# Keys and values spread to the score and value matmuls three phases ahead, keys by way of DRAM, values from SBUF to SBUF, and a one-instruction normalisation on GpSimd

## The reference

```python
# L0: pre-norm, causal self attention, cross attention, MLP
x = x + sdpa(split(ln(x, g1, b1) @ w_qkv.T), causal) @ w_prj1.T + b_prj1
x = x + sdpa(ln(x, g2, b2) @ w_q.T, ctx @ w_kv.T) @ w_prj2.T + b_prj2
x = x + gelu(ln(x, g3, b3) @ w_fc1.T + b_fc1) @ w_fc2.T + b_fc2
# L1: rms norm, rotary q and k, cross attention
x = x + sdpa(rope(rms(x) @ Wq.T), rope(ctx @ Wk.T), ctx @ Wv.T) @ Wo.T
# L2: post-norm, masked scores
x = ln(x + mha(x, x, causal) @ Wo1 + bo1, g1, b1)
x = ln(x + mha(x, ctx, mask) @ Wo2 + bo2, g2, b2)
x = ln(x + gelu(x @ W1 + bf1) @ W2 + bf2, g3, b3)
# L3: as L0 without a causal mask, norms without gain and bias
```

## Time and profile before

| | |
|---|---|
| runs (median) | 2578.21 us (2570.23 to 2578.39) |
| profiled execution, its own time | 2566.47 us |
| its span, first to last instruction | 2564.4 us |
| mean granted TensorE clock | 0.967 of 2.4 GHz |
| PE / PEld / DVE / ACT / POOL busy | 89 / 75 / 72 / 65 / 54 % |
| DMA | 231.55 MB, 90 GB/s, q1 30.4% of 16 engines |

### The profile page before, as it was taken

One profiled execution on the slowest core, in us unless ns is written; L12 is line 12 of the kernel. 1 busy time (PEld: TensorE's weight loads), 2 busy tenths in 40 slices (PEclk: granted clock), 3 DMA queues, 4 the chain that ended last, 5 costly groups with the idle time before them and its releaser, 6 DMA issues.

```text
span 2564.4 us, 98727 instructions
## 1 busy us (share of the span) xinstructions
PE 2276.3 (89%) x37613; PEld 1919.4 (75%) x37613; DVE 1852.0 (72%) x4653; ACT 1657.8 (65%) x2884; POOL 1390.3 (54%) x3557
## 2 busy tenths in 40 slices
PE   2689888999998897999999988899999989799987
PEld 2478776788887776778887777778888877678875
DVE  3368776777777777778776777677777777677863
ACT  0256654778776664677776765477777766467775
POOL 3244334877554433688654443487755543377843
PEclk6799999999999999999999999999999999999999
DMA  6133333333333333333333333333333322333321
GB/s 153 44 91 97 89 89 93 86 94 94 99 98 89 90 88 89 91 91 92 99 98 83 101 90 90 93 86 94 91 100 97 90 79 83 87 90 89 93 76 44
DMA packets 354629, 231.55 MB, mean 90 GB/s; under 512 B 151456, under 2 KB 295584, under 8 KB 354144
## 3 DMA queue, kind: packets, MB, share of 16 engines
q1 hardware_dynamic: 349152, 222.07, 30.4%
q10 hardware_dynamic: 4128, 1.65, 0.3%
q0 software_dynamic: 864, 1.28, 0.3%
HBM read 159.87 MB, written 65.01 MB: 88 GB/s over the span
## 4 chain that ended last, share of the span: by engine, by line
PE 34%; POOL 25%; issue 21%; DMA 13%; DVE 3%; SPq 2%; POOLq 1%; ACT 1%; DVEq 0%; ACTq 0%
DMA kv_dram<-qkv_rows 6%; PE ps_scores_t L825 6%; DMA k_slots<-kv_dram 6%; PE ps_out L813 5%; PE ps_scores L788 5%; PE ps_turn L873 3%; POOL x_bias L660 3%; PE ps_wide L895 3%; POOL pre_rstd L604 2%; POOL post_rstd L604 2%; PE ps_turn L878 2%; POOL post_normed L641 2%; POOL x L644 2%; PE ps_wide L853 2%; PE ps_wide L854 2%
## 5 line engine op out<-in xcount | busy, mean ns | idle before, releaser
L1118 DVE TENSOR_REDUCE row_max<-ps_scores 128x16 f32<-128x1024 f32 x448 | 548.6, 1224 | 444.1 <-PE ps_scores L788 259.4
L727 ACT ACTIVATE probs<-ps_scores_t 128x512 f32<-128x512 f32 x896 | 535.4, 598 | 168.0 <-PE ps_scores_t L825 165.8
L1124 DVE TENSOR_TENSOR shifted<-ps_scores,row_max 128x512 f32<-128x512 f32 x896 | 611.8, 683 | 16.0 <-issue 0.6
L825 PE MATMUL ps_scores_t<-ident,shifted 128*128 128x128 f32 x3584 | 572.9, 283 | 15.9 <-ACT probs L727 15.1
L788 PE MATMUL ps_scores<-k_slots,qkv_rows 32*64 32x256 f32 x7168 | 317.4, 409 | 200.4 <-DMA k_slots<-kv_dram 150.5
L717 ACT COPY pv_sb<-ps_out 128x256 f32<-128x256 f32 x448 | 167.1, 373 | 461.0 <-PE ps_out L813 458.0
L825 PEld LDWEIGHTS ps_scores_t<-ident,shifted 128*128 128x128 f32 x3584 | 398.5, 143 | 55.4 <-issue 21.6
L813 PEld LDWEIGHTS ps_out<-probs,v_ones 128*32 128x32 f32 x14336 | 278.6, 151 | 146.9 <-issue 146.9
L813 PE MATMUL ps_out<-probs,v_ones 128*32 128x64 f32 x14336 | 343.1, 237 | 4.8 <-issue 3.7
L788 PEld LDWEIGHTS ps_scores<-k_slots,qkv_rows 32*64 32x64 f32 x7168 | 108.9, 132 | 291.7 <-issue 195.6
L707 ACT COPY qkv_rows<-ps_wide 128x384 f32<-128x384 f32 x384 | 184.3, 480 | 132.8 <-PE ps_wide L863 129.2
(11 more groups left out here) (170 smaller groups left out, 4530.9 us busy)
## 6 DMA issues: line engine op xcount, KB each, us to landing
k_slots<-kv_dram SPq DMA_DIRECT2D x448, 256.0 KB, 3.0
kv_dram<-qkv_rows SPq DMA_DIRECT2D x384, 128.0 KB, 2.2
v_ones<-kv_dram SPq DMA_DIRECT2D x896, 32.0 KB, 2.6
kv_dram<-qkv_rows SPq DMA_DIRECT2D x128, 64.0 KB, 1.7
x_in<-in_x SPq DMA_DIRECT2D x64, 64.0 KB, 1.9
ctx_in<-in_ctx SPq DMA_DIRECT2D x64, 64.0 KB, 1.9
out<-x SPq DMA_DIRECT2D x64, 64.0 KB, 1.7
kv_dram<-zeros SPq DMA_DIRECT2D x4, 512.0 KB, 7.1
```

The costliest lines, as they stand in the source:

```text
L727: nc.scalar.activation(probs[:, u, :, :], ps_scores_t[:, :] .rearrange("p (h t) -> p h t", h=4), ACT.Exp, scale=SCALE).then_inc(probs_read ...
L825: ins = nc.tensor.transpose(ps_scores_t[:, h * P:(h + 1) * P], shifted[:, j % 2, u, h * P:(h + 1) * P], ident[:, :])
L1118: v.tensor_reduce(row_max[:, :].rearrange("p (g n) -> p g n", n=SLOTS), ps_scores[:, :, 0:256].rearrange("p g (n k) -> p g n k", k=LEN), A ...
L1124: v.tensor_tensor(shifted[:, j % 2, u, :].rearrange("p (g n k) -> p g n k", n=SLOTS, k=LEN), ps_scores[:, 2 * u:2 * u + 2, 0:256].rearrang ...
```

## The change

The phase constants: q, k and v are computed three phases ahead of the scores (QKV 2 to 3), turns four (TURN_IN 3 to 4), statistics six (STATS 4 to 6).

On SP, `spread` is split. `rows_out(j+QKV)` sends k's rows to DRAM (64 KB, now without v) and v by four DMAs from SBUF to SBUF (64 partitions by 1 KB each); `spread(j+QKV-1)`, ahead of it in the phase, waits for the k write of the phase before and reads the slots. v's rows are written by ACT into `v_rows`, which already holds the zeros and ones around them, in a ring of eight (FAR), and `v_ones` has the same layout, so that the 32 weight columns of a value matmul are adjacent. ACT's one copy becomes two. On DVE, half 1 of `shift` comes right after half 0. On POOL, `normalised` is a drain and one tensor_scalar with mean and inverse root as its two scalars. Two waits are added for the program's ends (POOL on turns_ready, PE on attn_ready).

```diff
-QKV, TURN_IN, STATS = 2, 3, 4
+QKV, TURN_IN, STATS = 3, 4, 6
...
-        qkv_rows = sb("qkv_rows", [P, RING, 3, P])
+        qk_rows = sb("qk_rows", [P, RING, 2, P])
+        v_rows = sb("v_rows", [P, FAR, 2, HEADS // 2, V_COLUMNS])
-        v_ones = sb("v_ones", [P, RING, 2, 32, HEADS // 2])
+        v_ones = sb("v_ones", [P, FAR, 2, HEADS // 2, V_COLUMNS])
...
+                def rows_out(r, j):
+                    c, f = j % RING, j % FAR
+                    rope = layer_of(j) == L1_CROSS
+                    if rope:
                         sp.wait_ge(rope_ready.sem, rope_ready.at(r, j))
+                    else:
+                        sp.wait_ge(rows_ready.sem, rows_ready.at(r, j, 1))
+                    sp.dma_start(k_rows(c)[:, K_HOME:], qk_rows[:, c, 1, :]).then_inc(k_written[c].sem, 16)
+                    if rope:
                         sp.wait_ge(rope_v_ready.sem, rope_v_ready.at(r, j))
                     else:
                         sp.wait_ge(rows_ready.sem, rows_ready.at(r, j))
+                    for e in range(2):
+                        for b in range(2):
+                            sp.dma_start(v_ones[64 * e:64 * e + 64, f, b, :, :], v_rows[64 * b:64 * b + 64, f, e, :, :]) \
+                                .then_inc(v_landed[f].sem, 16)
+
+                def spread(r, j):
+                    c = j % RING
+                    sp.wait_ge(k_written[c].sem, k_written[c].at(r, j))
                     sp.dma_start(k_slots[:, c, :, :], k_windows(c)).then_inc(k_landed[c].sem, 16)
...
                 def phase(r, j, this, following):
+                    if exists(r, j + QKV - 1):
+                        spread(r, j + QKV - 1)
                     if exists(r, j + QKV):
-                        spread(r, j + QKV)
+                        rows_out(r, j + QKV)
...
                 def normalised(r, j, norm, src, rms=False):
+                    pool.drain()
+                    if rms:
+                        return pool.tensor_scalar(norm.normed[:, b, :], src, norm.rstd[:, b:b + 1], None, ALU.mult)
+                    return pool.tensor_scalar(norm.normed[:, b, :], src, norm.mean_var[:, b, 0:1],
+                                              norm.rstd[:, b:b + 1], ALU.subtract, ALU.mult)
...
                 def copy_rows(r, j):
-                    nc.scalar.copy(qkv_rows[:, j % RING, :, :], ps_wide[:, 0:3 * P]
-                                   .rearrange("p (n t) -> p n t", t=P)).then_inc(rows_ready.sem, 1)
+                    nc.scalar.copy(qk_rows[:, j % RING, :, :], ps_wide[:, 0:2 * P].rearrange("p (n t) -> p n t", t=P)) \
+                        .then_inc(rows_ready.sem, 1)
+                    nc.scalar.copy(v_pairs(j % FAR), ps_wide[:, V_COLS].rearrange("p (e h d) -> p e h d", e=2, d=HD)) \
+                        .then_inc(rows_ready.sem, 1)
...
-                                                       v_ones[:, c, b, :, 4 * u + h],
+                                                       v_ones[:, f, b, 4 * u + h, :],
...
                     if exists(r, j):
                         maxima(r, j)
                         shift(r, j, 0)
+                        shift(r, j, 1)
                     if has_mlp(r, j - DOWN):
                         mlp_residual(r, j - DOWN)
                     if exists(r, j - OUT):
                         residual(r, j - OUT)
                     if rope:
                         rope_products(r, j + QKV)
-                    if exists(r, j):
-                        shift(r, j, 1)
```

More of the change, by code:

```diff
@@ L313, in build @@
         rope_ready = signal("rope_ready", {L1_CROSS: 1})
-        twice = {n: 32 if n == L1_CROSS else 16 for n in range(LAYERS)}
-        kv_written = [signal(f"kv_written{c}", twice, RING) for c in range(RING)]
+        k_written = [signal(f"k_written{c}", 16, RING) for c in range(RING)]
         k_landed = [signal(f"k_landed{c}", 16, RING) for c in range(RING)]
-        v_landed = [signal(f"v_landed{c}", 32, RING) for c in range(RING)]
+        v_landed = [signal(f"v_landed{c}", 64, FAR) for c in range(FAR)]
         zeroed = sem("zeroed")
@@ L324, in build @@
         gelu_ready = signal("gelu_ready", with_mlp)
-        rows_ready = signal("rows_ready", {n: 1 for n in range(LAYERS) if n != L1_CROSS})
+        rows_ready = signal("rows_ready", {n: 2 for n in range(LAYERS) if n != L1_CROSS})
         rope_v_ready = signal("rope_v_ready", {L1_CROSS: 1})
-        post_rstd = signal("post_rstd", {n: 5 for n in POST_NORM})
-        mlp_rstd = signal("mlp_rstd", {n: 3 for n in MLP_PRE_NORM})
-        mlp_post_rstd = signal("mlp_post_rstd", {n: 5 for n in MLP_POST_NORM})
+        post_rstd = signal("post_rstd", {n: 4 for n in POST_NORM})
+        mlp_rstd = signal("mlp_rstd", {n: 2 for n in MLP_PRE_NORM})
+        mlp_post_rstd = signal("mlp_post_rstd", {n: 4 for n in MLP_POST_NORM})
         post_x_ready = signal("post_x_ready", {n: 1 for n in POST_NORM})
@@ L334, in build @@
         mlp_h_ready = signal("mlp_h_ready", {n: MLP_H_STEP for n in MLP_PRE_NORM})
-        pre_rstd = signal("pre_rstd", {n: 2 if n == L1_CROSS else 3 for n in PRE_NORM})
+        pre_rstd = signal("pre_rstd", {n: 2 for n in PRE_NORM})
         pre_norm = Norm(sb, "pre", PRE_NORM, pre_steps, pre_rstd)
@@ L344, in k_windows, with k_rows, v_pairs @@
         def k_windows(c):
[L347 to L353, removed]
+            rows = k_dram[c, K_HOME:K_HOME + P * K_ROW]
+            return bass.AP(tensor=rows.tensor, offset=rows.offset,
+                           ap=[[SLOTS * K_ROW, P // SLOTS], [K_ROW - P, SLOTS], [1, SLOTS * P]])
+        def k_rows(c):
+            return k_dram[c, 0:P * K_ROW].rearrange("(p x) -> p x", x=K_ROW)
+        def v_pairs(f):
+            wide = v_rows[:, f, :, :, :]
+            step = wide.ap[1][0] + HD
+            return bass.AP(tensor=wide.tensor, offset=wide.offset, ap=[wide.ap[0], [step, 2], wide.ap[2], [1, HD]])
         x_dram = a["x"].rearrange("(r n two) t c -> r n (two t) c", two=2, n=STREAMS)
@@ L621, in pre_norm_end @@
                     if layer in PRE_NORM:
+                        if isinstance(r, int):
+                            pool.wait_ge(turns_ready.sem, turns_ready.at(r, j - RING - TURN_IN))
                         inverse_root(r, j, pre_norm)
@@ L962, in _ @@
                 v = nc.vector
-                for rows, one, zero in ((slice(0, 64), 16, 24), (slice(64, 128), 24, 16)):
-                    v.memset(v_ones[rows, :, :, one:one + HD, :], 1.0).then_inc(setup_mem, 1)
-                    v.memset(v_ones[rows, :, :, zero:zero + HD, :], 0.0).then_inc(setup_mem, 1)
-                    v.memset(v_ones[rows, :, :, 24 - one:32 - one, :], 0.0).then_inc(setup_mem, 1)
+                for e in range(2):
+                    for at, value in ((HD - HD * e, 0.0), (2 * HD + HD * e, 1.0), (3 * HD - HD * e, 0.0)):
+                        v.memset(v_rows[:, :, e, :, at:at + HD], value).then_inc(setup_mem, 1)
                 wait_first_loads(dve)
```

64 lines of the change are left out of this document (26 added, 38 removed).

## The result

| | before | after |
|---|---|---|
| runs, median | 2574.41 us (2570.23 to 2578.39, 4 runs) | 2391.26 us (2388.54 to 2399.85, 4 runs) |
| ratio | | 0.9294, 95% interval 0.9262 to 0.9326 |
| profiled execution, its own time and its span | 2566.5, 2564.4 us | 2388.5, 2386.7 us |
| mean granted TensorE clock | 0.967 | 0.983 |

What follows compares the result with a forecast made beforehand. PE, 89% busy, was taken as nearly the bound, held up mainly by k_slots. Windows -127, fill -23, clock -15, drain -3 and costs +6 were taken as -163: own time 2403, median 2412 us; 8 in 10 for 2335 to 2500.

Steps and rivals of the forecast that it cites:

- The seven windows: Stretches of 16 units, 137 to 734 us: 597 us fall to 564, 33 less a round, -127 in all.
- the fill: First 8 units, 82 us, paced by DRAM hops: each unit 2.9 us shorter, -23 us.
- the costs of ACT and rope: ACT's second copy 6 us, rope V matmul's wait 16 us, partly in the busy time already: +6 together.
- The value matmuls: Adjacent v_ones weight columns on PE: 0 to 0.24 us a unit could be won, taken as 0.
- Rival 2: Value matmuls get faster too, 30 to 107 us more: 0.15 us a unit, 67 us, total 2345; chance 0.16.
- The norm: POOL's subtract and multiply become drain and one instruction: 0.5 us, between 0.19 and 1.6, hidden by the spare phase.
- The statistics' phase: STATS 6 against TURN_IN 4 gives POOL's norms a phase more: the 10.3 us waits on pre_normed go.
- The moved shift: DVE's second shift before the residuals: 29.7 us of score waits go, 16 us of rope V matmul waits come.
- Rival 3: SP becomes the bound, slower: decides at 1.08 us a v issue, some 2800 us at 1.3; chance 0.05.
- ACT's two copies: ACT's one 384-column copy becomes 256 and 128: ends 0.03 us later, mlp_up waits 6 us, at most 38.
- Rivals 1 and 4: 1: rope windows stay long, 2492 us, chance 0.14; 4: k_slots stays late behind v, 2525 us, chance 0.05.
- the prediction's own list of signs: Included k_slots wait under 10 us, PE 93% or more, windows 77 to 86 us, v issues under 0.45 us.

Runs made afterwards that it cites:

- the strided run: Value matmuls take their 32 weight columns 8 elements apart from the same v_ones, against the changed kernel: 2414.52 us, ratio 0.9356 to the kernel before.
- the run with half of v: The two v DMAs of the second sequence left out (four SP issues a phase for six), against the changed kernel: 2381.15 us, ratio 0.9275 to the kernel before.

## Why the prediction was right, and where it wasn't

**The seven windows and the fill.** Forecast -33 us a round, measured -37, -38 and -34 in the three rounds. From the scores of the 9th unit to the last it is -151; that holds the clock's gain and the costs of ACT and rope too, forecast together as -127-15+6 = -136. k no longer waits, as the earlier trace rows let expect: 138 of 150 us went. The method was to take PE's busy time plus 2 us a window. It held because PE did become the bound outside the stretch of post-norms, and because it takes all of PE's smaller waits at once: the sum didn't rest on the single terms below. The fill gave -29 for -23 (81.6 to 52.4 us for 8 units), at a granted clock of 0.88 where it was 0.73. Over the span the clock went from 0.967 to 0.983.

**The value matmuls: the term of the sum that was mis-sized.** I took 0 for a range of 0 to 0.24 us a unit. It is 0.10 us of PE in each group (0.68 to 0.58), 42 us of busy time and 21 us of device time by the strided run. Rival 2 was true in its mechanism, and its price of 67 us three times too high: the eight rounds of 20 ns gave 0.15 us a unit, and half of the gain in busy time is lost to waits. The load fell to 110 ns, below the 132 of the scores' 64 columns that I had taken as its neighbour. The note on "cachelines" in the Trainium skill's SBUF — State Buffer page, that each access crossing into a new 16-byte line pays, agrees in its direction: 151 against 110 ns for 32 columns, 32 bytes apart or adjacent; the runs don't show that it is the cause.

**The norm: wrong in size and in what hides it.** "I take 0.5 ... The spare phase hides it." It takes 0.80 us and 0.19 us of drain, more than the pair with its overlap, and costs 33 us. The bounds held (0.19 to 1.6), the value didn't. And POOL, to which the prediction gave a chance of 0.02 as the bound, is the bound in one stretch of each round. "POOL is busy 66 of 82 us" was read as room. In the trace before, the part of that window with four norms in two phases already had no pause in it; at 0.17 us more a norm the two phases take the 11.7 us that POOL takes. The spare phase of STATS doesn't help there: it is for pre-norms alone, and the distance from a post-norm's or the MLP norm's statistics to the turn that reads them was not changed. The phrase in the Trainium skill's GPSIMD Engine Reference (4.1), "1-input is roughly line-rate", is not borne out here: the instruction with one tensor input and two scalars takes 801 ns, that with two tensor operands, one of them a broadcast, 401.

**The statistics' phase: right in sign, far too small.** "The 10.3 us go" counted the wait in the old schedule. In the new one the phase is worth 69 us with the old norm and 100 with the new. So at five phases POOL's norms end last, in L2 above all; why they didn't in the kernel before is argued, not shown. The sum escaped the error, since it went by PE's busy time with all waits gone.

**The moved shift: a gain of 30 us counted, none seen.** The 29.7 us of `shifted` went and 36 us of waits for DVE's x came (14.3, 11.8 and two of 5); the forecast had 16, from 0 to 60. Undone, nothing changes in either version of the norm.

**SP.** Forecast 0.34 us a v issue, measured 0.59 in the median, inside the bounds (0.17 to 1.98), and 2.39 at most, outside; that makes 3.7 us of a phase for 2.5. That is hidden, by the run with half of v. The DMA engines stand at 0.50 to 0.54 of their time in these windows where 0.4 was forecast. Rival 3's point of decision lies between the two loads that were run: four issues a phase don't set the pace, eight do; where between wasn't looked for.

**ACT's two copies: about as forecast.** They follow each other after 0.27 us where I took 0.14, and the pair ends 0.06 us later than the one copy did (0.27+0.27 for 0.48), where 0.03 was taken. What waits is the weight load ahead of mlp_up's first matmul, before and after:

```profile
PEld ps_wide L892 <- ACT qkv_rows L707: 24.0, 147, 0.6
```

```profile
PEld ps_wide L909 <- ACT v_rows L723: 35.8, 169, 0.2
```

These are 12 us more of waits of the load. The matmul itself starts 0.04 us later behind the one ahead of it (235 ns for 198, in the mean of 192 phases): 7 us, for a forecast of 6. No run undid this part.

**Rivals 1 and 4** are out: the L1 windows are 82 and 76 us, and k is on time.

So the total missed by 21 us: the span by 14 (2386.7 for 2401), 15 of them behind the fill and 6 in it, less 4 by which the first scores come later (at 59.2 us for 55.0) and small terms; the rest is that the median lay 3 us above the profiled execution's own time and not 9. Inside the windows the gain of the weights (21) and the loss of the norm (33) nearly cancel, and neither was in the forecast. That the total came out so near is luck to this extent. By the prediction's own list of signs it was half right: PE's share (93%) and the L1 windows came, the k wait (12.6 us) came near, the v issues (0.59 us) and the load of v_ones (110 ns) didn't, and one sign of being wrong did, the group of v_ones below 0.6 us (0.58).

## What to carry to other kernels

Bound a pipeline by the busy time of its fullest engine plus the small idle share that a bound window shows; single waits of the old schedule don't price the parts of a change, since a wait that is small beside a large stall (10 us) can be worth 70 to 100 once the stall is gone. Before one instruction replaces two on an engine, measure it: fewer instructions was 46 us more of busy time here. A mean busy share doesn't tell whether an engine has room: POOL at 66 of 82 us was an engine with no pause in the part of the window that counted, so look in the timeline for the longest stretch without one. And check for each use whether the slack that is to hide it exists there: a distance that was widened for one norm leaves the others as they were.

## What the runs showed of the hardware

- On GpSimd a tensor_scalar of 128x128 fp32 with two per-partition scalars takes some 800 ns (801 to 836 by its tile) and with one 612, a tensor_tensor with one operand a broadcast scalar 401, with two full tensors 457. A drain ahead of it leaves 0.19 us idle.
- A weight load of 32 fp32 columns takes 110 ns when they are adjacent and 151 when they lie 32 bytes apart; the group of 32 matmuls behind them 0.58 and 0.68 us.
- A DMA from SBUF to SBUF costs its queue's engine 0.59 us to issue in the median, for 32 partitions as for 64, and up to 2.4.
